# Turning the queries and keys of a three-layer attention kernel with one sixteen-block transposing DMA a visit

## The chip, the core and the metric

The kernel runs on one NeuronCore of a Trainium2 chip. The engines are PE (TensorE, matrix products), DVE (VectorE), ACT (ScalarE), POOL (GpSimd) and SP (SyncE, which here only issues DMAs). Each engine works through its own instructions in order, and they wait for one another by semaphores. The metric is the time of one execution on the device, in microseconds (us), lower being better.

## What is computed

Eight sequences of 128 tokens with 144 channels pass a rotation that depends on a condition vector, and then three transformer blocks with 16 heads of 9 channels and a hidden width of 576. Shifts, scales and gates of each block come from the same condition vector. Blocks 1 and 2 use a layer norm, block 3 an RMS norm, and block 3 also normalises queries and keys per head.

```python
x = _L0_cond_ref(x, cond, P, W, b)               # rotation: expm of a skew matrix, per sequence
...
h = _modulate(_layernorm(x), shift_msa, scale_msa)
qkv = (h @ W_qkv + b_qkv).reshape(b, l, 3, H, D)  # H = 16, D = 9
q, k, v = (qkv[:, :, 0], qkv[:, :, 1], qkv[:, :, 2])
scores = jnp.einsum('blhd,bmhd->bhlm', q * scale, k)
attn = jax.nn.softmax(scores, axis=-1)
o = jnp.einsum('bhlm,bmhd->blhd', attn, v).reshape(b, l, c)
x = x + gate_msa * (o @ W_proj + b_proj)
h = _modulate(_layernorm(x), shift_mlp, scale_mlp)
x = x + gate_mlp * (gelu(h @ W_fc1 + b_fc1) @ W_fc2 + b_fc2)
```

## The kernel before

The first third of the time is a preparation: loads, condition products, a matrix exponential and an orthogonalisation with one small step after another on DVE. After that come 24 **visits**, one for each sequence in each layer (visit v is sequence v % 8 of layer v // 8). Visits of equal parity share buffers (index h = v % 2).

**One visit.** TensorE turns the normalised tokens (`h_turn`) and makes queries, keys and values into PSUM bank 1 (`qkv`). Queries and keys are needed to better than bf16, so each number is written as three bf16 parts: ACT writes the first part (`first`, k = 0 for the queries and 1 for the keys), DVE the remainder (`residue`, `second_parts`, `third_parts`). The parts of a head pair fill one block of 128 by 128, so that a visit has 16 blocks, 8 of queries and 8 of keys. They lie in `brief` with the tokens on partitions and have to be turned, into `skw_r`, before `scores` can multiply them. `scores(v, g)` with g = 0 and g = 2 makes eight products each into banks 6 and 7, DVE takes the row maxima of every four heads (`maxima(v, 0)` to `maxima(v, 3)`), splits them (`max_high`, `max_low`), TensorE turns them (`max_turn`), and `scores_T` makes the transposed scores less the maxima; ACT takes the exponential (`exps`), `pv` multiplies with the values, `o_back`, `o_turn` and `proj` bring the result back, and the gated sum goes into x. The feed-forward half (`h2_turn`, `fc1`, `gelu`, `fc2`, `mlp_out`) is done for two visits at a time.

**How the blocks are turned.** Three ways share the 16 blocks. TensorE turns blocks 0 to 3 (queries of heads 0 to 7) by four transposing products into bank 6 (`parts_turn`, line 1309) and DVE copies them out (`q_out`, line 1971). SP turns blocks 12 to 15 by one DMA (line 375), which are the keys of heads 0 to 7, because the weights' columns are rolled by half the keys (`by_head` on the host). SP turns blocks 4 to 11 by a second DMA (line 376). `scores(v, 0)` needs the copy and the first DMA only, `scores(v, 2)` the second one. SP issues both when `third_parts` has signalled `parts_ready` and the buffer of two visits before is free.

**What sets the order.** The visits overlap. Each engine runs a loop over slots from -2 to 27, and a table written by hand lists, for each kind of slot (the first two, even and odd ones of layers 1 and 2, even and odd ones of layer 3, the last ones), which step of which visit stands next in the engine's queue: in slot s TensorE does `scores` of visit s, `scores_T` and `pv` of visit s - 1, `qkv` of visit s + 1, and so on. An even and an odd slot together are called a pair here; a pair is two visits. `stay_warm(n)` puts n products into the queue whose result is never read.

Of the kernel before, what the change touches and what calls it, by code (L numbers as in the profile page):

```python
# [37 lines left out]
H, HD = 16, 9  # L38
# [79 lines left out]
def program(nc, t, out, spread_mods):  # L118
    ctx = ExitStack()
    with ctx:  # L120
# [117 lines left out]
        qkT = [[both_turned[h][:, 8 * k:8 * k + 8, :] for h in range(2)] for k in range(2)]  # L238
# [55 lines left out]
        qT_full, qT_ready = sem("qT_full"), sem("qT_ready")  # L294
        keys_turned = [sem(f"keys_turned{h}") for h in range(2)]
# [30 lines left out]
        def _(sp):  # L326
# [85 lines left out]
        def _(pool):  # L412
# [189 lines left out]
            for slot in range(-2, VISITS + 4):  # L602
                if slot < 2 and slot % 2 == 0:
                    pair_at(second_half_tail, slot, 4, 0)
                    visit_at(first_deviation, slot + 2, start=2)
                    pair_at(mlp_add, slot, 6)
                    visit_at(attention_add, slot - 2)
                    visit_at(first_tail, slot + 2, start=2)
                    pair_at(second_half_tail, slot, 4, 1)
                elif slot < 2 and slot % 2 == 1:  # L610
                    pair_at(second_deviation, slot, 3)
# [3 lines left out]
                elif slot >= VISITS - 1 and slot % 2 == 0:  # L615
                    visit_at(last_parts, slot - 3, start=LAST)
                    visit_at(first_deviation, slot + 2, start=2)
                    pair_at(second_half_tail, slot, 4, 0)
                    pair_at(second_half_tail, slot, 4, 1)
                    visit_at(attention_add, slot - 2)  # L620
                    visit_at(first_tail, slot + 2, start=2)
                    visit_at(last_deviation, slot - 2, start=LAST)
                    pair_at(mlp_add, slot, 6)
                elif slot >= VISITS - 1 and slot % 2 == 1:
                    visit_at(first_deviation, slot + 2, start=2)
                    visit_at(last_parts, slot - 3, start=LAST)
                    visit_at(attention_add, slot - 2)
                    pair_at(second_deviation, slot, 3)
                    visit_at(first_tail, slot + 2, start=2)
# [1781 lines left out]
```

## Time and profile before

| | us |
|---|---|
| median of 3 runs | 363.49 |
| lowest and highest run | 363.12, 363.57 |
| the profiled execution, its whole time | 363.12 |
| its span, first to last instruction | 361.2 |
| PE, DVE, ACT, POOL busy in the span | 308.4, 293.4, 207.2, 166.2 |

The profiled execution took 1.9 us outside its span. The visits begin at about 113 us. Visits 2 to 15 (layers 1 and 2) run in pairs of 17.6 us until about 248 us, visits 16 to 23 (layer 3) in pairs of 20.6 to 20.7 us until about 331 us, and the rest is the end of the last visits.

How to read the rows: the name left of the arrow is what an instruction writes and the one right of it what it reads (`ps` is PSUM, `brief` the parts, `skw_r` the turned parts, `nmax` the maxima), L followed by a number is a line of the kernel (L1016 is a helper for most products, L375 and L376 are the two transposing DMAs), and xN is how often. PEld is the load of a product's stationary operand. SPq is SP's queue.

### The profile page before, as it was taken

The page shows a single profiled execution, that of the slowest core. Times are in us where ns is not written, and L with a number is a line of the kernel's source. Part 1 is how long each engine was busy: PE and PEld are TensorE (multiplying, and loading weights), DVE is VectorE, ACT ScalarE, POOL GpSimd, SP SyncE. Part 2 cuts the span into 40 slices and gives each one's busy share as a digit, 9 for nine tenths or more (in the row PEclk, how much of TensorE's full clock was granted, in tenths as well). Part 3 has the DMA queues.
Part 4 walks back from the last instruction along what each step waited for, and adds up shares of the span by engine and source line. Part 5 has one row for each costly group of instructions (what it writes and reads, how often), then busy time and mean ns, then how long its engine had stood idle before and what let it go on. Part 6 is the DMA issues. An engine that isn't in the chain of part 4 may idle for free.

```text
span 361.2 us, 10726 instructions
## 1 busy us (share of the span) xinstructions
PE 308.4 (85%) x3494; PEld 211.6 (59%) x3502; DVE 293.4 (81%) x1511; ACT 207.2 (57%) x460; POOL 166.2 (46%) x536
## 2 busy tenths in 40 slices
PE   1969983983668998799999999999999998989896
PEld 0924721472124455486878777777666675766675
DVE  4999999999995678787888888787989888887632
ACT  4145110244011365688888887888686867768552
POOL 5424332356553322535354545454646646452442
PEclk9987655697699999999999999999999999999999
DMA  4797400039300233223222222222023222223101
GB/s 147 185 255 234 126 1 0 4 80 291 117 1 0 45 60 76 45 45 46 45 44 48 45 45 48 44 47 46 15 45 32 45 47 45 45 41 37 34 16 34
DMA packets 48735, 23.58 MB, mean 65 GB/s; under 512 B 40186, under 2 KB 47198, under 8 KB 48552
## 3 DMA queue, kind: packets, MB, share of 16 engines
q1 hardware_dynamic: 48680, 22.89, 27.8%
q8 instruction: 29, 0.48, 0.5%
q14 instruction: 26, 0.21, 0.2%
HBM read 12.82 MB, written 0.62 MB: 37 GB/s over the span
## 4 chain that ended last, share of the span: by engine, by line
PE 42%; DVE 39%; issue 8%; DMA 4%; POOL 3%; SPq 1%; ACT 1%; POOLq 0%; DVEq 0%
PE ps L1016 34%; DMA skw_r<-brief 4%; DVE grow L1647 4%; DVE nmax L1976 3%; DVE top L1702 3%; DVE trow L1647 3%; PE ps L1415 3%; DVE beta L1681 3%; DVE den L1687 2%; DVE tfac L1695 2%; DVE lead L1669 2%; DVE late L1669 2%; PE ps L1309 1%; DVE gfac L1663 1%; DVE grec L1659 1%
## 5 line engine op out<-in xcount | busy, mean ns | idle before, releaser
L1976 DVE TENSOR_REDUCE nmax<-ps 128x4 f32<-128x512 f32 x96 | 63.4, 683 | 11.7 <-PE ps L1016 11.4
L796 ACT ACTIVATE skw_t<-ps 128x512 f32<-128x512 f32 x96 | 52.0, 595 | 14.8 <-PE ps L1016 14.2
L448 POOL TENSOR_TENSOR root<-grow,half 32x1 f32<-32x1 f32 x64 | 34.6, 542 | 54.0 <-DVE grow L1647 53.6
L1016 PE MATMUL ps<-skw_r 54*128 54x128 bf16 x768 | 43.5, 217 | 4.7 <-DMA skw_r<-brief 2.3
L1016 PEld LDWEIGHTS ps<-skw_r 54*128 54x128 bf16 x768 | 30.4, 94 | 20.8 <-issue 11.5
L1016 PE MATMUL ps<-mT_t,fc1w_t 128*128 128x256 f32 (+1 forms) x130 | 36.0, 379 | 0.0
L1016 PE MATMUL ps<-fc2w,skw_r 128*128 128x144 f32 (+1 forms) x240 | 34.7, 292 | 0.0
L1016 PE MATMUL ps<-sel,identb 128*128 128x512 bf16 x83 | 23.7, 404 | 9.6 <-DVE grow L1647 8.6
L1016 PEld LDWEIGHTS ps<-fc2w,skw_r 128*128 128x128 f32 (+1 forms) x240 | 30.8, 190 | 1.6 <-issue 0.2
L1016 PE MATMUL ps<-nmT,sel 64*128 64x128 bf16 x384 | 27.6, 216 | 0.0
L813 ACT ACT_TABLE_LOAD x21 | 26.9, 1283 | 0.4
L562 POOL TENSOR_TENSOR rstd<-vare,nhalf 128x1 f32<-128x1 f32 x24 | 13.2, 552 | 28.8 <-DVE vare L2075 18.6
L548 POOL TENSOR_TENSOR tail<-ln,gmod 128x16 f32<-128x16 f32 x48 | 12.0, 250 | 29.3 <-DVE ln L1883 23.9
L1016 PEld LDWEIGHTS ps<-mT_t,fc1w_t 128*128 128x128 f32 x130 | 18.9, 190 | 5.9 <-issue 2.0
L1016 PE MATMUL ps<-qkvw_t,hT_t 128*128 128x432 f32 x48 | 22.3, 545 | 0.0
L557 POOL TENSOR_TENSOR x<-x,skw_r 128x144 f32<-128x144 f32 x24 | 11.8, 490 | 22.4 <-DVE skw_r L2025 22.4
L790 ACT ACTIVATE brief<-ps 128x432 bf16<-128x432 f32 x32 | 16.9, 562 | 7.8 <-PE ps L1016 7.8
L1016 PE MATMUL ps<-skw_t,brief 128*32 128x128 f32 x512 | 19.8, 278 | 1.0 <-DVE skw_r L2025 0.4
L1016 PEld LDWEIGHTS ps<-sel,identb 128*128 128x128 bf16 x91 | 7.7, 101 | 21.1 <-DVE grow L1647 9.3
L828 ACT ACTIVATE skw_r<-ps 128x512 f32<-128x512 f32 (+1 forms) x33 | 16.7, 515 | 5.8 <-PE ps L1016 5.7
L1016 PEld LDWEIGHTS ps<-nmT,sel 64*128 64x128 bf16 x384 | 19.6, 94 | 0.0
L803 ACT ACTIVATE skw_t<-ps 128x512 f32<-128x512 f32 x24 | 14.0, 583 | 7.0 <-PE ps L1016 6.9
(273 smaller groups left out, 815.4 us busy)
## 6 DMA issues: line engine op xcount, KB each, us to landing
gmod<-spread_mods SPq DMA_DIRECT2D x3, 1408.0 KB, 13.2
adaw_t<-in_ada SPq DMA_DIRECT2D x3, 432.0 KB
tails<-in_tail SPq DMA_DIRECT2D x3, 427.1 KB
skw_t<-in_skw SPq DMA_DIRECT2D x1, 1024.0 KB
fc1w_t<-in_fc SPq DMA_DIRECT2D x3, 320.0 KB
fc2w<-in_fc SPq DMA_DIRECT2D x3, 288.0 KB
skw_r<-brief SPq DMA_TRANSPOSE x48, 3.1
qkvw_t<-in_qkv SPq DMA_DIRECT2D x3, 216.0 KB
```

The source lines that it names most:

```text
L448: g.tensor_tensor(root[:, p, j:j + 1], grow[:, i % 4, 0:1], half[:], ALU.pow).then_inc(root_ready, 1)
L548: step(g.tensor_tensor(y[:], ln[kind][h][:, 128:C], m[:, CT:2 * CT], ALU.mult))
L562: g.tensor_tensor(rstd[:, 0, h:h + 1], vare[:, 0, h:h + 1], nhalf[:, 0:1], ALU.pow).then_inc(rstd1, 1)
L790: a.activation(dst, src, ACT.Copy).then_inc(first_parts, 1)
L796: a.activation(prob[g].rearrange("p i t -> p (i t)"), ps[:, 2 + g % 2, :], ACT.Exp, scale=SCALE).then_inc(prob_ready, 1)
L803: a.activation(o_raw[v % 2].rearrange("p g t -> p (g t)"), ps[:, 4, :], ACT.Copy).then_inc(o_raw_ready, 1)
L813: a.activation(table_out[:], half[:], f).then_inc(table_used, 1)
L828: a.activation(hid[0:rows, 2 * r:2 * r + n, :, :].rearrange("p c h t -> p (c h t)"), ps[0:rows, FC1_BANKS[r], 0:n * 2 * T], f).then_inc(hi ...
L1016: return pe.matmul(o, lhsT, rhs, start=start, stop=stop, skip_group_check=True)
L1647: return d.stream_shuffle(out_, rows, [j] * HALF)
L1669: i = d.scalar_tensor_tensor(out=elim[p][:, w], in0=grow[:, (HALF * p + j) % 4, 1:D + 1], scalar=gfac[:, p, j:j + 1], in1=elim[p][:, w], o ...
L1976: d.tensor_reduce(nmax[:, v % 2, first:first + 7:2], ps[:, 6 + g % 2, :].rearrange("p (i t) -> p i t", i=4), AX_X, ALU.max, negate=True).t ...
```

## The change

All 16 blocks of a visit are turned by one DMA. The four transposing products of TensorE, the copy of DVE, the rolled key columns and the semaphores `qT_full`, `qT_ready` and `keys_turned` are gone. `scores(v, 0)` now waits for the whole DMA, and `scores(v, 2)` for nothing more. `first` waits for the DMA of two visits before instead of its three sources. The unread products before the first scores fall from 8 and 8 to 6 and 2, and the two before `parts_turn(1)` go. The tables of all slots are rewritten on all four engines.

```diff
@@ -372,8 +371,7 @@
                 sp.wait_ge(parts_ready, v + 1)
                 if v >= 2:
                     sp.wait_ge(sT_full, 4 * (v - 2) + 4)
-                sp.dma_start_transpose(both_turned[h][:, 12:16, :], both_parts[h][:, 12 * T:16 * T]).then_inc(keys_turned[h], 16)
-                sp.dma_start_transpose(both_turned[h][:, 4:12, :], both_parts[h][:, 4 * T:12 * T]).then_inc(turned[h], 16)
+                sp.dma_start_transpose(both_turned[h], both_parts[h]).then_inc(turned[h], 16)
...
@@ -776,10 +774,6 @@
                 if v >= 2:
-                    if k == 0:
-                        act.wait_ge(qT_full, v - 1)
-                    else:
-                        act.wait_ge(keys_turned[h], 16 * (v // 2))
                     act.wait_ge(turned[h], 16 * (v // 2))
...
@@ -1300,16 +1294,6 @@
-            def parts_turn(v):
-                if v == 1:
-                    stay_warm(2)
-                o = refill(6, qT_ready, v + 1).bitcast(BF16)
-                pe.wait_ge(parts_ready, v + 1)
-                for pair in range(H // 4):
-                    i = pe.transpose(o[:, pair * T:(pair + 1) * T],
-                                     parts[0][v % 2][:, 2 * pair:2 * pair + 2, :].rearrange("p h d -> p (h d)"), identb[:])
-                i.then_inc(qT_full, 1)
-
...
@@ -1359,13 +1343,10 @@
             def scores(v, g):
                 if v == 0:
-                    stay_warm(8)
+                    stay_warm(6 - 2 * g)
                 if v == 1:
                     stay_warm(1 + g)
                 if g == 0:
-                    pe.wait_ge(qT_ready, v + 1)
-                    pe.wait_ge(keys_turned[v % 2], 16 * (v // 2 + 1))
-                else:
                     pe.wait_ge(turned[v % 2], 16 * (v // 2 + 1))
...
@@ -1964,12 +1937,6 @@
-            def q_out(v):
-                dve.wait_ge(qT_full, v + 1)
-                if v >= 2:
-                    dve.wait_ge(sT_full, 4 * (v - 2) + 4)
-                d.tensor_copy(qkT[0][v % 2][:, 0:4, :].rearrange("p k t -> p (k t)"), ps[:, 6, :].bitcast(BF16)[:, 0:4 * T]).then_inc(qT_ready, 1)
-
```

One entry of the tables, of DVE's even slots in layers 1 and 2, shows how the orders move:

```diff
...
                 elif slot % 2 == 0:
                     visit_at(input_stats, slot + 3, start=2)
-                    visit_at(input_means, slot + 3, start=2)
+                    visit_at(residue, slot + 1, start=1)
+                    visit_at(gated, slot - 2)
                     visit_at(maxima, slot, 0)
...
```

TensorE's queue in an even slot of layers 1 and 2, before: the turned maxima (L1385), the tokens, the four transposes (L1309), then eight products of `scores_T` (read from `skw_r` and `nmT`) and `o_back` (L1415).

```order
397 L1385 MATMUL ps<-identb,nmp 128x128
398 L1251 MATMUL ps<-ident,ln 128x128
399 L1241 MATMUL ps<-identb,tailp 102x128
400 L1309 MATMUL ps<-identb,brief 128x128 x4
401 L1016 MATMUL ps<-skw_r 128x128 x2
```

Further on in the same slot, before: the end of `scores_T`, then `scores(v, 0)` (the row of x8), then `proj`.

```order
420 L1016 MATMUL ps<-skw_r 128x128 x2
421 L1016 MATMUL ps<-nmT,sel 128x128 x2
422 L1016 MATMUL ps<-skw_r 128x128 x8
423 L1016 MATMUL ps<-projw_t,x_t 128x144
424 L1016 MATMUL ps<-projw_u,x_t 128x144
```

The same two places in one piece, after.

```order
412 L1010 MATMUL ps<-skw_r 128x128 x2
413 L1010 MATMUL ps<-nmT,sel 128x128 x2
414 L1010 MATMUL ps<-projw_t,x_t 128x144
415 L1010 MATMUL ps<-projw_u,x_t 128x144
416 L1010 MATMUL ps<-skw_r 128x128 x8
```

The four transposes are gone, and `scores(v, 0)` stands behind `proj` instead of ahead of it; odd slots are changed in the same way.

DVE's queue in an odd slot of layers 1 and 2, before, from the second maxima to the parts of the next visit: `maxima` (L1976), the statistics of `second_input` (L1864 to L1870), two `maxima`, `residue` (L1953), `max_high` (L1989), `second_parts` (L1960), `max_low` (L1994), `third_parts` (L1965).

```order
962 L1976 TENSOR_REDUCE nmax<-ps 128x4
963 L1864 BN_STATS st<-x 128x6 x2
964 L1867 BN_AGGR st<-st 128x2 x2
965 L1870 TENSOR_SCALAR vare<-st 128x2
966 L1976 TENSOR_REDUCE nmax<-ps 128x4 x2
967 L1953 TENSOR_TENSOR res<-ps,brief 128x288
968 L1989 CAST nmp<-nmax 128x2x8
969 L1960 CAST brief<-res 128x16x2x9
970 L1960 CAST brief<-res 128x16x18
971 L1994 TENSOR_TENSOR nmp<-nmax,nmp 128x2x8
972 L1965 TENSOR_TENSOR brief<-res,brief 128x2x16x9
```

The same place, after.

```order
944 L1943 TENSOR_REDUCE nmax<-ps 128x4 x2
945 L1837 BN_STATS st<-x 128x6 x2
946 L1840 BN_AGGR st<-st 128x2 x2
947 L1843 TENSOR_SCALAR vare<-st 128x2
948 L1943 TENSOR_REDUCE nmax<-ps 128x4
949 L1926 TENSOR_TENSOR res<-ps,brief 128x288
950 L1933 CAST brief<-res 128x16x2x9
951 L1933 CAST brief<-res 128x16x18
952 L1938 TENSOR_TENSOR brief<-res,brief 128x2x16x9
953 L1943 TENSOR_REDUCE nmax<-ps 128x4
```

The parts of the next visit are finished ahead of the fourth maxima and of their split; in even slots they stand behind the first two maxima both before and after.

## Rows read from the trace of the kernel before

**Rows 1.** Windows, one pair each; columns: us, busy time by engine, PEclk, DMA

```profile
177.60:195.20 17.60, 17.38 (x241) 13.41 (x240) 14.38 (x48) 14.83 (x32) 8.81 (x30) 1.00 0.24 48
...
289.60:310.30 20.70, 19.15 (x242) 13.81 (x244) 18.34 (x68) 15.54 (x35) 11.84 (x40) 1.00 0.20 40
```

**Rows 2.** The chain of waits, from 130 us; columns: start, duration, what

```profile
141.36 4.96 DMA skw_r<-brief
...
160.08 6.92 PE ps L1016 x107
...
178.34 6.92 PE ps L1016 x107
...
195.94 6.92 PE ps L1016 x107
...
281.25 4.62 DMA skw_r<-brief
...
289.53 0.30 PE ps L1236
...
310.23 0.30 PE ps L1236
```

**Rows 3.** Groups by line and form, 141 to 246 us (12 visits)

```profile
L1309 PE MATMUL ps<-identb,brief 128*128 128x128 bf16 x47 | 4.6, 219 | 0.0
L1971 DVE COPY skw_r<-ps 128x512 bf16<-128x512 bf16 x12 | 5.0, 415 | 0.0
```

**Rows 4.** The two DMAs by source line, all visits: duration of the issue, landing

```profile
L375 SPq DMA_TRANSPOSE skw_r<-brief x24: 1189/1191/1309, 120.9 to 330.7; - x24
...
DMA to landing us min/median/max: 2.4/2.4/4.3
```

**Rows 5.** The same for the DMA of eight blocks

```profile
L376 SPq DMA_TRANSPOSE skw_r<-brief x24: 1297/1312/2483, 122.2 to 332.0; - x24
...
  PEld ps L1016: 6.6, 8
...
DMA to landing us min/median/max: 3.1/3.2/5.0
```

**Rows 6.** DMA windows of one visit's two transfers; columns as in rows 1

```profile
203.90:204.70 0.80, 0.80 (x11) 0.69 (x6) 0.41 (x3) 0.75 (x3) 0.53 (x3) 1.00 0.81 164
205.10:206.70 1.60, 1.48 (x28) 0.88 (x26) 1.20 (x7) 1.17 (x4) 1.23 (x7) 1.00 0.86 164
```

**Rows 7.** Timeline of an odd and an even slot; columns: start, duration, instruction

```profile
196.40 0.40 PE L1016 MATMUL ps<-skw_r 54*128 54x128 bf16 x8
...
198.44 0.52 DVE L1864 BATCH_NORM_STATS2 st<-x 128x6 f32<-128x144 f32 x2
...
202.24 0.46 DVE L1965 TENSOR_TENSOR brief<-res,brief 128x288 bf16<-128x288 f32 x1
...
202.73 1.19 SPq L375 DMA_TRANSPOSE skw_r<-brief  x1
...
203.96 1.31 SPq L376 DMA_TRANSPOSE skw_r<-brief  x1
...
206.50 0.39 PE L1016 MATMUL ps<-skw_r 54*128 54x128 bf16 x8
...
206.92 0.69 DVE L1976 TENSOR_REDUCE nmax<-ps 128x4 f32<-128x512 f32 x1 [0.56 <-PE ps L1016]
...
209.50 0.45 DVE L1965 TENSOR_TENSOR brief<-res,brief 128x288 bf16<-128x288 f32 x1
```

**Rows 8.** Landing of single visits: line 375 at 133.4, line 376 at 332.0

```profile
DMA to landing us min/median/max: 3.1/3.1/3.1
...
DMA to landing us min/median/max: 4.0/4.0/4.0
```

**Rows 9.** Timeline of TensorE, first visits

```profile
123.49 0.40 PE L1016 MATMUL ps<-skw_r 54*128 54x128 bf16 x8 [0.40 <-issue]
...
125.65 0.40 PE L1016 MATMUL ps<-skw_r 54*128 54x128 bf16 x8
```

More of the change, by code:

```diff
@@ new lines, in _ @@
+                    pair_at(mlp_add, slot, 6)
+                    visit_at(last_parts, slot - 2, start=LAST)
+                elif slot >= VISITS - 1 and slot % 2 == 1:
+                    visit_at(first_tail, slot + 2, start=2)
+                    visit_at(attention_add, slot - 2)
+                    visit_at(first_deviation, slot + 2, start=2)
+                    visit_at(last_deviation, slot - 2, start=LAST)
+                    visit_at(last_parts, slot - 2, start=LAST)
+                elif (slot + 1) // B == 2 and slot % 2 == 0:
+                    pair_at(second_deviation, slot, 4)
@@ L995, in _ @@
                     pair_at(gelu, slot, 4, 0)
-                    pair_at(gelu, slot, 4, 1)
-                    visit_at(v_out, slot + 1, start=1)
-                else:
+                else:
+                    pair_at(gelu, slot, 5, 1)
+                    visit_at(v_out, slot, start=1)
                     pair_at(gelu, slot, 5, 2)
@@ L1008, in _ @@
                     visit_at(exps, slot - 1, 3)
-                    visit_at(v_out, slot + 1, start=1)
                     visit_at(o_out, slot - 1)
@@ new lines, in _ @@
+                    visit_at(scores_T, slot - 1, 2)
+                    visit_at(scores, slot, 0)
+                    pair_at(fc1, slot, 4, 0)
+                    visit_at(pv, slot - 1, 2)
+                    pair_at(fc1, slot, 4, 1)
+                    visit_at(o_back, slot - 2)
+                    visit_at(scores, slot, 2)
+                    visit_at(proj, slot - 2)
+                    visit_at(pv, slot - 1, 3)
+                elif slot < 2 and slot % 2 == 1:
+                    visit_at(h_turn, slot + 1, start=2)
+                    visit_at(o_back, slot - 2)
+                    visit_at(qkv, slot + 1, start=1)
+                    pair_at(fc1, slot, 5, 2)
+                    visit_at(max_turn, slot - 1)
+                    pair_at(fc2, slot, 5, 0)
+                    visit_at(scores, slot, 0)
+                    visit_at(scores_T, slot - 1, 0)
+                    visit_at(scores_T, slot - 1, 2)
+                    visit_at(scores, slot, 2)
@@ L1443, in _ @@
                     visit_at(pv, slot - 1, 0)
                     visit_at(pv, slot - 1, 1)
+                    visit_at(o_turn, slot - 2)
+                    pair_at(fc2, slot, 5, 1)
+                    visit_at(proj, slot - 2)
+                    visit_at(pv, slot - 1, 2)
+                    visit_at(pv, slot - 1, 3)
+                elif slot >= VISITS - 1 and slot % 2 == 0:
+                    visit_at(scores, slot, 0)
+                    visit_at(h_turn, slot + 1, start=2)
+                    visit_at(o_back, slot - 2)
@@ L2156, in _ @@
                     visit_at(attended, slot - 1)
[L2157 removed]
+                    pair_at(second_input, slot, 3)
+                    visit_at(gated, slot - 2)
                 elif slot >= VISITS - 1 and slot % 2 == 0:
+                    visit_at(next_normal, slot + 2, start=2)
                     visit_at(input_stats, slot + 3, start=2)
[L2160 to L2161 removed]
+                    visit_at(residue, slot + 1, start=1)
```

418 lines of the change are left out of this document (179 added, 239 removed).

## Prediction

> **What bounds the kernel now.** I read the busy time by stretch first. In a pair of layers 1 and 2 TensorE is busy 17.38 of 17.60 us, DVE 14.38, ACT 14.83 [rows 1]: TensorE is the bound. In a pair of layer 3 TensorE is busy 19.15 and DVE 18.34 of 20.70 us [rows 1]: neither is full, and the chain of waits runs from one to the other and through POOL. The granted clock is 1.00 in both. The chain of waits then gives the lengths. The same piece of TensorE work starts at 160.08, 178.34 and 195.94, so one pair took 18.26 us and the next 17.60 [rows 2]; in layer 3 the mark at 289.53 comes again at 310.23, 20.70 us later [rows 2]. Last I read what each transposing DMA takes, since the change rests on that.
>
> **The transfer.** The DMA of four blocks lands 2.4 us after its issue began (median), that of eight 3.1 us [rows 4, 5]. The second is issued 1.23 us after the first (202.73 and 203.96 [rows 7]), so all blocks are there 4.3 to 4.4 us after the parts are ready. In the windows the packets of the four blocks fill 0.8 us from 1.17 us after the issue, those of the eight 1.5 to 1.6 us, at 164 GB/s over each window [rows 6]; the landing is about 0.5 us after the last packet. Sixteen blocks by the step from four to eight (0.7 us for four blocks): 3.1 + 2 x 0.7 = 4.5. By the windows: 1.2 + 2 x 1.5 + 0.5 = 4.7. I take 4.6 us, with bounds of 4.2 (one start-up less than the two windows hold) and 5.0. So the last block comes 0.2 us later than now, but the operands of `scores(v, 0)` come at 4.6 instead of 2.4.
>
> **A page's rate.** By the packets the transposing transfers ran at 164 GB/s over the windows [rows 6]. The Trainium skill, Advanced Engine Details and Errata, section X-Bar Transpose (TRN2), expects 350 to 400 GB/s of such a transfer. By that the 524 kB of sixteen blocks would take about 1.4 us and land after some 3.1 us (an estimate from that page and the start and end above), and no wait named below would be left. The rows say 164, and I go by them.
>
> **What is removed.** Per visit the four transposing products go. Their group shows 4.6 us for 47 of them in twelve visits, 0.38 us a visit with the pipeline's tail, which the next product overlaps [rows 3]; their starts are about 0.06 us apart, 0.24 us for four. I take 0.25 us of TensorE a visit, 0.5 a pair, between 0.5 and 0.8. DVE loses the copy, 0.415 us a visit [rows 3]: worth nothing in layers 1 and 2, where DVE idles 3.2 us a pair, and up to 0.8 us a pair in layer 3. SP loses one issue of 1.3 us a visit, which delays nobody now but the landing already counted.
>
> **Layers 1 and 2.** TensorE alone would make the pair 17.60 - 0.5 = 17.1 us. Moving `proj` ahead of `scores(v, 0)` may add 0.1 us a slot, because `proj` waits for ACT's copy and the scores used to fill that gap; moving `max_turn` up takes the same back from the wait for the turned maxima. I put both at nothing. Now the other loop, by which parts go to the DMA, the DMA to the scores, and DVE reaches the next parts only behind the maxima of these scores. In an even slot the scores start at 206.50, the first maxima at 206.92 [rows 7], so 0.42 us; then two maxima of 0.65, two casts in 0.52 and `third_parts` 0.45: 2.8 us from landing to issue. In an odd slot `second_input` (about 1.05 us from 198.44 [rows 7]), the third maxima and `residue` stand between as well: 0.42 + 1.3 + 1.05 + 0.9 (the third maxima, with its wait for the second scores) + 0.45 + 1.0 = 5.1 to 5.2 us. With two landings: 2.8 + 5.2 + 2 x 4.6 = 17.2 us. Before, the same loop was 206.50 to 209.95, 196.40 to 202.70 [rows 7] and twice 2.44: 14.6 us, which leaves 3.0 us of slack in a pair of 17.6. **This slack is what hides a late transfer today, and the change spends all of it.** The pair becomes 17.2 us, a gain of 0.4; for seven pairs -2.8 us.
>
> **Late transfers.** They are common. Read visit by visit, ten of the 24 visits have a landing at least 0.7 us over the median of its kind; the first is 3.1 instead of 2.4 at visit 2, the last 4.0 instead of 3.1 at visit 23 [rows 8], the largest 4.3 instead of 2.4 and 5.0 instead of 3.1 [rows 4, 5]. By the larger of a visit's two excesses they sum to 12.6 us, 5.9 of it in visits 2 to 15 and 6.7 in layer 3. What of it is paid now: the 4.96 us landing at 141.36 is on the chain, 1.8 us over the median, and the pair from 160.08 is 0.66 us over its neighbour [rows 2]: 2.5 us. In layer 3 the 4.62 at 281.25 is on the chain too [rows 2], but pairs with and without such a piece are equally long, so I count nothing as paid. In all, the weight loads waited 6.6 us for the second DMA in eight cases [rows 5]. With a loop of 17.2 against TensorE's 17.1 a late landing is paid in full. How many will be late is the unknown. The excess is no property of the transposes' own length (fourteen visits have none), so the same number of delays met by a transfer that is 0.3 us longer in all bounds it near 12.6; half of it if the moved transfers miss what they met before. I take two thirds, 8.4 us, less 2.5 paid now: **+5.9 us** (bounds +3.8 and +10.1; 0 or below if the landings are clean).
>
> **Layer 3.** The same loop: even slot 0.42 + 1.3 + `unit_parts` 0.52 + ACT's `first` with its wait 1.3 + 0.45 + 1.1 = 5.1; odd slot, with `second_normal`, the other two maxima and their split, 6.1; with two landings 5.1 + 6.1 + 9.2 = 20.4 us against 20.70 now. TensorE falls to 18.65 and DVE to 17.5, so neither takes over. I take -0.25 us a pair, -1.0 for four, between -3.2 (the copy of DVE and the transposes in full) and +1.
>
> **The first and the last visits.** Visit 0 has its first scores at 123.49 and the second at 125.65, as the second DMA lands [rows 9]. Now both start at about 125.4, behind the whole transfer, and two `maxima` of 0.65 us that ran between them come after: +1.3, less the unread products of 0.4 us that also go, +0.9 us. The two `parts_turn` of the start, 0.25 each less what waits cover, give back 0.2. Sum +0.7, between -0.5 and +1.5. The end needs the last blocks of visit 23, whose DMA lands 4.0 us after 332.0 [rows 8], that is 5.3 after the parts; 4.6 to 6 then, at no cost and no gain. `gelu` and `v_out` cross into the next slot on ACT, which idles 2.8 us a pair, and `attention_add` goes behind `first_tail` on POOL, which is half idle: nothing, since `second_input` comes later on DVE; if that cover is gone, 0.5 us of POOL's add appears once a pair.
>
> **The sum.** -2.8 - 1.0 + 0.7 + 5.9 = +2.8 us on the profiled execution, 361.2 of span and 1.9 around it, 363.12 in all: 365.9. The median is 0.37 above that execution, so I predict **366.3 us**.
>
> **The rivals.**
>
> *Clean landings, faster.* If the sixteen blocks land after 4.6 us or less nearly always, the late term is not +5.9 but -2.5, since today's delays go too: -2.8 - 1.0 + 0.7 - 2.5 = -5.6, **357.9 us**; with a third of the excess (+1.7 net) it is about 362. For it speaks that fourteen of 24 visits have no delay, that one DMA can be hit only once, and that both full engines lose work. It decides at a late excess of about 5.6 us in all: below, the kernel is faster. A landing of 4.2 us adds 0.8 us of slack a pair and has the same effect. The skill's rate, above, would end here as well.
>
> *Even, no change.* Half of the excess is met (6.3 - 2.5 = +3.8): -2.8 - 1.0 + 0.7 + 3.8 = +0.7, **364.2 us**, and with a little less it is 363.5.
>
> *Full exposure.* All of the 12.6 us is paid: -2.8 - 1.0 + 0.7 + 10.1 = +7.0, **370.5 us**. A landing of 5.0 us would do the same: 0.8 us a pair in eleven pairs, +8.8. Against it: the queue orders have been moved so that parts come earlier and scores later, which the loop sums above may hold by 0.3 us too high.
>
> **How the numbers follow.** Two executions of this kernel differ by about 0.2%, 0.7 us, and less than that can't be told from no change. The forecast with full exposure, that is slower by over 0.2%: 0.48, of it 0.12 for above 369. Even: 0.14. Clean landings, faster by over 0.2%: 0.38. The slower case alone spans 364.3 to 371. Because both signs hold much, the range takes in both: it reaches from 358.5, which leaves out some 0.09 of the clean end, to 371.0, which leaves out 0.06 above.
>
> **What would show it.** The transposing DMA: 24 issues of about 1.5 us, landing at 4.6 in the median (4.2 and 5.0 decide for the rivals), and a maximum near 6. The forecast is right if the weight loads' waits for that DMA grow from 6.6 us to over 12 in all, and pairs of layers 1 and 2 fall apart into some of 17.2 us and some of 18 to 19. It is wrong if all of them are 17.2 or less, with those waits under 4 us: then the parts come earlier than my loop has them. DVE should be 10 us less busy, TensorE 6 to 10 less. If layer 3's pairs leave 20.4 by more than 1 us in either direction, the step on layer 3 has failed; if the first scores of visit 0 start before 125 us, the landing has.

## The result and the profile after

The changed kernel takes **383.80 us** (median of 4 runs, 380.32 to 385.62), the kernel before in its company 363.31 us (363.12 to 363.57): ratio **1.055**, 95% interval 1.051 to 1.058 (here and below a ratio leaves out runs over 1.5% above the fastest of the same kernel, a median takes in all). I had said 366.3 us and at most 371. The direction was right, the size was not. The profiled execution took 384.43 us with a span of 382.6 us, 21.4 us more than before.

Where do the 21.4 us lie? The issue of a visit's first transposing DMA is a good mark. That of visit 3 comes 7.1 us later than before (147.3 for 140.1 us), the stretch from there to visit 15 is 7.7 us longer (112.7 for 105.0), that from visit 15 to 23 is 5.5 us longer (91.1 for 85.6), and the rest adds 1.1. So there are three questions: first visits, pairs of layers 1 and 2, layer 3.

First the page, the busy time and granted clock of the changed kernel:

```profile
PE 316.5 (83%) x3396; PEld 211.7 (55%) x3396; DVE 288.2 (75%) x1487; ACT 207.4 (54%) x460; POOL 163.6 (43%) x536
...
PEclk9988555895999669799999999999999999989999
```

TensorE lost its 96 transposing products and is busy 8.1 us longer than before. The dips to 6, 6 and 7 behind 124 us and to 8 behind 335 us are part of the answer: in the kernel before, the clock was 1.00 throughout these stretches.

The DMA by its source line, which answers [rows 4, 5]:

```profile
L374 SPq DMA_TRANSPOSE skw_r<-brief x24: 1784/1912/3107, 121.1 to 351.1; - x24
...
  PEld ps L1010: 11.1, 11
  PE ps L1010: 8.3, 7
...
DMA to landing us min/median/max: 4.2/4.3/6.0
```

The median landing is 4.3 us, 0.3 less than forecast, with a tail to 6.0. TensorE's products stood idle for it seven times, its weight loads waited eleven times, eight of them in visits 16 to 23, that is in every visit of layer 3.

**First visits.** The timeline of TensorE (idle time before the instruction in brackets), then all stretches of the changed kernel behind 120 us in which the granted clock was 0.50 (the column before the last two):

```profile
125.46 0.40 PE L1010 MATMUL ps<-skw_r 54*128 54x128 bf16 x8 [2.95 <-DMA skw_r<-brief]
127.33 0.61 PE L1010 MATMUL ps<-skw_r 54*128 54x128 bf16 x8 [0.93 <-DVE nmax L1943]
```

```profile
127.37:141.02 13.65, 11.46 (x105) 6.69 (x105) 6.93 (x21) 5.10 (x12) 2.41 (x8) 0.50 0.23 44
151.26:158.09 6.83, 6.65 (x71) 3.60 (x69) 5.37 (x16) 3.23 (x7) 2.07 (x7) 0.50 0.01 2
335.58:338.99 3.41, 3.17 (x31) 2.59 (x32) 2.90 (x10) 2.03 (x4) 2.10 (x9) 0.50 0.00 0
```

The first scores start at 125.46, as forecast (125.4; before at 123.49 [rows 9]). But TensorE had stood still for 2.95 us, and soon after it ran for 13.7 us at the lower of its two levels (1.2 instead of 2.4 GHz). The same happens at 151 us, behind a wait of 1.69 us for the split maxima, and at 336 us in layer 3.

**Pairs of layers 1 and 2.** Marks from the chain of waits, a window of one pair (answers [rows 1, 2]), and the only waits of TensorE's products over 0.2 us in it:

```profile
177.99 1.69 PE ps L1010 x19
...
196.82 1.69 PE ps L1010 x19
```

```profile
177.99:196.82 18.83, 17.79 (x235) 13.22 (x236) 14.09 (x45) 14.63 (x32) 8.72 (x30) 1.00 0.30 58
```

```profile
180.69 0.48 PE L1010 MATMUL ps<-projw_t,x_t 128*128 128x144 f32 x2 [0.23 <-ACT x_t L829]
196.06 0.22 PE L1366 MATMUL ps<-identb,nmp 128*128 128x128 bf16 x1 [0.81 <-DVE nmp L1961]
```

A pair is 18.83 us long instead of 17.60, and no DMA is among the waits: one waits for ACT's copy in front of `proj`, one for the split maxima in front of `max_turn`. Of the 1.23 us, 0.41 is busy time (17.79 for 17.38) and 0.82 idle time of TensorE.

**Layer 3.** The chain of waits has the late landings in it:

```profile
304.88 5.99 DMA skw_r<-brief
...
317.28 5.66 DMA skw_r<-brief
...
328.00 5.90 DMA skw_r<-brief
```

TensorE waited 4.4 us for these three, 1.48 of it in visit 21:

```profile
333.95 0.34 PE L1010 MATMUL ps<-skw_r 54*128 54x128 bf16 x6 [1.48 <-DMA skw_r<-brief]
```

Behind this one the clock falls for 3.4 us (the third window above). In each of the visits 16 to 22 the first scores start at most 0.06 us behind the landing, so that here, unlike in layers 1 and 2, the landing is in the loop and a late one is paid in full. The pairs from issue to issue are 20.9, 22.0 and 24.4 us, against 20.5 to 20.8 before.

### The profile page after: what moved, and what is told of

Same layout as the page of the kernel before. It is cut to its first block, busy times and chain, and to the rows that moved or that the text cites. A ratio compares the mean times of both kernels' runs of the same rounds, so it can differ in the third digit from the quotient of the medians.

```text
span 382.6 us, 10388 instructions
## 1 busy us (share of the span) xinstructions
PE 316.5 (83%) x3396; PEld 211.7 (55%) x3396; DVE 288.2 (75%) x1487; ACT 207.4 (54%) x460; POOL 163.6 (43%) x536
## 4 chain that ended last, share of the span: by engine, by line
DVE 38%; PE 38%; DMA 11%; issue 7%; ACT 3%; POOL 2%; SPq 1%; POOLq 0%; ACTq 0%; DVEq 0%
PE ps L1010 32%; DMA skw_r<-brief 10%; DVE nmax L1943 5%; DVE grow L1620 3%; DVE top L1675 3%; DVE trow L1620 3%; DVE beta L1654 2%; PE ps L1396 2%; DVE den L1660 2%; DVE tfac L1668 2%; DVE brief L1933 2%; DVE late L1642 2%; DMA tmask<-in_tmask 1%; DVE lead L1642 1%; DVE tnum L1661 1%
## 5 line engine op out<-in xcount | busy, mean ns | idle before, releaser
L1943 DVE TENSOR_REDUCE nmax<-ps 128x4 f32<-128x512 f32 x96 | 62.3, 684 | 14.4 <-PE ps L1010 13.9
L1010 PE MATMUL ps<-skw_r 54*128 54x128 bf16 x768 | 47.7, 226 | 14.8 <-DMA skw_r<-brief 8.3
L1010 PEld LDWEIGHTS ps<-skw_r 54*128 54x128 bf16 x768 | 30.8, 98 | 33.5 <-DMA skw_r<-brief 11.1
L1010 PE MATMUL ps<-fc2w,skw_r 128*128 128x144 f32 (+1 forms) x240 | 35.6, 297 | 0.0
L1010 PEld LDWEIGHTS ps<-fc2w,skw_r 128*128 128x128 f32 (+1 forms) x240 | 31.9, 194 | 3.9 <-issue 3.3
L1010 PE MATMUL ps<-nmT,sel 64*128 64x128 bf16 x384 | 28.8, 222 | 0.0
L546 POOL TENSOR_TENSOR tail<-ln,gmod 128x16 f32<-128x16 f32 x48 | 11.0, 228 | 37.8 <-DVE ln L1856 28.4
L1010 PE MATMUL ps<-qkvw_t,hT_t 128*128 128x432 f32 x48 | 25.1, 606 | 0.8 <-issue 0.8
L1010 PE MATMUL ps<-skw_t,brief 128*32 128x128 f32 x512 | 20.6, 287 | 0.4
L822 ACT ACTIVATE skw_r<-ps 128x512 f32<-128x512 f32 (+1 forms) x33 | 17.1, 517 | 7.1 <-PE ps L1010 7.1
L836 ACT ACTIVATE hT_t<-ps,mod_t 128x128 f32<-128x128 f32 x24 | 10.9, 455 | 14.1 <-PE ps L1235 14.1
```

The source lines that it names most:

```text
L822: a.activation(hid[0:rows, 2 * r:2 * r + n, :, :].rearrange("p c h t -> p (c h t)"), ps[0:rows, FC1_BANKS[r], 0:n * 2 * T], f).then_inc(hi ...
L1010: return pe.matmul(o, lhsT, rhs, start=start, stop=stop, skip_group_check=True)
L1943: d.tensor_reduce(nmax[:, v % 2, first:first + 7:2], ps[:, 6 + g % 2, :].rearrange("p (i t) -> p i t", i=4), AX_X, ALU.max, negate=True).t ...
```

## The experiments

The comparison with the kernel before is in each case with its runs in the same company (medians 362.2 to 364.0 us). Two theories stood at the start: the orders cost the time (A), or the longer transfer does (B).

**1. Only the fills of the first visits.**

```diff
-                    stay_warm(6 - 2 * g)
+                    stay_warm(20 - 7 * g)
```

> The changed kernel with more unread products ahead of the first scores (20 and 13 instead of 6 and 2), so that TensorE works through the 2.9 us and 0.9 us it idled behind the first transfer. Theory clock: the idle time at 122.5 to 125.5 us let the granted clock fall to 0.5 until 140 us and again at 150 us; with it filled the clock stays at 1.00, and of the 7.2 us that visit 3's transfer starts later than before, about 4 come back: 379 to 380 us. Theory transfer (the first visits are late because each waits for its whole transfer, whatever the clock): 383 us, unchanged.

381.57 us, ratio 1.049 (1.044 to 1.054), 17.6 us above before instead of 20.5. The DMA of visit 3 is issued at 142.8 instead of 147.3 us, so the fall of the clock behind visit 0 had cost 4.5 us. A second fall from 145 us on takes a part of it back, and the total stays 1.6 us above the 379 to 380 us that I had expected. Idle TensorE and the clock behind it are shown as the cause of the first part.

**2. Only DVE's odd table:** `max_high` and `max_low` ahead of `mlp_out`, among the parts.

```diff
+                    visit_at(maxima, slot, 3)
                     visit_at(residue, slot + 1, start=1)
+                    visit_at(max_high, slot)
                     visit_at(second_parts, slot + 1, start=1)
+                    visit_at(max_low, slot)
                     visit_at(third_parts, slot + 1, start=1)
-                    visit_at(maxima, slot, 3)
                     pair_at(mlp_out, slot, 5)
-                    visit_at(max_high, slot)
-                    visit_at(max_low, slot)
```

> The changed kernel with one table changed: in DVE's odd slots of layers 1 and 2 the fourth maxima and the split of the maxima stand again ahead of and between the steps that write the parts, as before the change. Theory queue: TensorE's max_turn waited 0.8 us a pair for the split, and scores_T and all behind it with it; pairs go from 18.84 to 17.6 or less and the whole to about 376 us. Theory transfer: parts are now ready 0.7 us later, the transfer lands behind the place of the scores, and the pair stays near 18.8: 383 us.

380.02 us, ratio 1.042 (1.036 to 1.048). Pairs of 18.4 us: the wait of 0.81 us for the maxima was worth 0.44 us a pair. The 0.8 us that are left above 17.60 have another cause.

**3. The old orders with the one DMA of sixteen blocks.**

```diff
-                sp.dma_start_transpose(both_turned[h][:, 12:16, :], both_parts[h][:, 12 * T:16 * T]).then_inc(keys_turned[h], 16)
-                sp.dma_start_transpose(both_turned[h][:, 4:12, :], both_parts[h][:, 4 * T:12 * T]).then_inc(turned[h], 16)
+                sp.dma_start_transpose(both_turned[h], both_parts[h]).then_inc(turned[h], 16)
```

> The kernel before with all its orders as they were, and only the transposition changed: one DMA of sixteen blocks, no transposes by TensorE, no copy by DVE. Theory orders (most of the 20 us is from the rewritten tables): faster than the changed kernel, 366 to 372 us, and pairs of layers 1 and 2 at 17.6 to 18.2. Theory transfer (the landing of 4.3 us itself costs the 20 us, and the new tables soften it): slower than 384 us, pairs over 19 us.

**397.58 us**, ratio 1.090 (1.082 to 1.097). Theory A in its simple form fell: the new orders are worth 14 us. The chain of waits of one pair shows why:

```profile
200.76 4.28 DMA skw_r<-brief
...
205.08 3.60 PE ps L1009 x33
...
211.41 4.26 DMA skw_r<-brief
...
219.20 4.35 DMA skw_r<-brief
```

From 200.76 to 219.20 is 18.44 us, with two landings in it and 9.9 us of other steps. The kernel before had the same loop at 14.6 us, 9.8 us beside two landings of 2.4. Lengthening each by 1.9 gives 18.4. The 14 us that the new orders give back don't lie in these pairs (18.83 us with them) but mostly in layer 3: from the issue of visit 16 to that of visit 22 experiment 3 takes 78.2 us, the changed kernel 67.3, the kernel before 62.0. A part of that is the clock: around waits of 1.98, 2.94 and 2.99 us TensorE ran at 1.2 GHz for 6.8, 6.8 and 10.2 us there, and in the changed kernel for 3.4.

**4. Experiments 1 and 2 together.**

> The changed kernel with both edits, more unread products at the start and the split of the maxima first. If the two causes are independent, the gains add: 383.8 - 4 - 7.5 = about 372 us. If the clock's fall comes from later waits as well, less than the sum.

377.86 us and not 372, ratio 1.038 (1.033 to 1.043). A window of one pair, and the wait at its start:

```profile
209.50:227.90 18.40, 17.73 (x231) 13.20 (x232) 13.44 (x45) 14.62 (x33) 8.75 (x31) 1.00 0.31 60
```

```profile
209.50 0.63 PE L1396 MATMUL ps<-ident,skw_t 128*128 128x128 f32 x4 [0.44 <-ACT skw_t L797]
```

No DMA is waited for, and still 18.40 us. The new order has `o_back` in front of `scores_T(v, 0)` and waits there for ACT's copy, and TensorE's own busy time is 0.35 us longer than before [rows 1], although four blocks a visit are gone.

**5. The old orders with a short first transfer.** The eight blocks of the first scores become neighbours (the queries' columns are rolled, not the keys') and go first. The diff is against experiment 3.

```diff
-                sp.dma_start_transpose(both_turned[h], both_parts[h]).then_inc(turned[h], 16)
+                sp.dma_start_transpose(both_turned[h][:, 4:12, :], both_parts[h][:, 4 * T:12 * T]).then_inc(eight_turned[h], 16)
+                sp.dma_start_transpose(both_turned[h][:, 0:4, :], both_parts[h][:, 0:4 * T]).then_inc(turned[h], 16)
+                sp.dma_start_transpose(both_turned[h][:, 12:16, :], both_parts[h][:, 12 * T:16 * T]).then_inc(turned[h], 16)
```

> The kernel before with all its orders; no block is turned by TensorE, and the sixteen go in three transposing DMAs: the eight blocks that scores(v, 0) needs first (the queries' columns are rolled so that they are neighbours), then four, then four. Theory that the landing in front of the first scores is the direct cost: with an 8-block landing of 3.1 us instead of 4.3 the DMA loop is 14.6 + 2 x (3.1 - 2.4) = 16.0 us a pair, under TensorE's own work of about 17.1, so pairs of layers 1 and 2 come to 17.1-17.4 us and the kernel to 358-364 us. Rival, that TensorE's transposes were needed whatever the DMA's length is (SyncE's queue now issues three DMAs of 1.2 us, and the last blocks come late for scores(v, 2)): pairs stay at 18 us or more and the kernel above 370 us.

367.31 us, ratio 1.010 (1.004 to 1.016): 30 us less than experiment 3 with the same work on TensorE. This is the strongest single piece of evidence for theory B: in the old orders the length of the first landing is the cost. A window of a pair, and a group in it with TensorE's idle time before it:

```profile
178.85:196.29 17.44, 17.01 (x235) 12.88 (x235) 13.80 (x44) 14.84 (x32) 8.80 (x31) 1.00 0.34 63
```

```profile
L1013 PE MATMUL ps<-skw_r 54*128 54x128 bf16 x66 | 3.7, 217 | 0.2 <-DVE nmT L1972 0.2
```

The pair is 17.44 us. TensorE's busy time fell by 0.37 us, the pair by 0.16: the turned blocks had covered the wait of `scores_T` for the turned maxima, which now shows with 0.2 us. The pair had been expected at 17.1 to 17.4 us, the total at 358 to 364, and that it missed. Most of the loss, 3.5 of 5.9 us in the profiled execution, lies in one place of layer 3, visit 19 to 20, 15.2 us for 11.7. Timeline and window there:

```profile
294.50 0.40 PE L1013 MATMUL ps<-skw_r 54*128 54x128 bf16 x8 [1.66 <-DMA skw_r<-brief]
```

```profile
297.00:301.00 4.00, 4.00 (x42) 3.54 (x34) 2.39 (x9) 2.14 (x4) 1.45 (x5) 0.50 0.00 0
```

The landing was late (4.6 for 3.3 us), TensorE stood 1.66 us, and behind it ran at 1.2 GHz. A wait of 1.36 us in visit 21 was followed by no such fall. In layer 3 of the changed kernel waits of 1.57 and 1.33 us were not either, but one of 1.48 us was.

**6. The new orders with the short first transfer** (experiment 4 with the three DMAs of experiment 5).

> The changed kernel with the longer fills and the split ahead of mlp_out (as in the run with both), all new orders kept, but with the eight blocks for scores(v, 0) in a DMA of their own, then four and four. Theory that the new orders of TensorE are what costs 0.8 us a pair in layers 1 and 2 and the transfer no longer does: pairs stay at 18.3-18.5 us there; only the first visits and the late landings of layer 3 gain, 3-6 us, so 372-375 us. Theory that the landing still costs directly: pairs fall to 17.6 us or less, and the kernel to 366 us or less.

373.67 us, ratio 1.028 (1.025 to 1.032). The window of a pair, and the group of the `qkv` products in it, then that group of the kernel before (178 to 195 us):

```profile
182.49:200.89 18.40, 17.73 (x233) 13.20 (x235) 13.45 (x44) 14.62 (x32) 8.75 (x31) 1.00 0.31 59
```

```profile
L1014 PE MATMUL ps<-qkvw_t,hT_t 128*128 128x432 f32 x4 | 2.0, 578 | 0.0
```

```profile
L1016 PE MATMUL ps<-qkvw_t,hT_t 128*128 128x432 f32 x4 | 1.8, 526 | 0.0
```

18.40 us, to the hundredth what experiment 4 had with landings 1 us longer. So in layers 1 and 2 the landing costs the changed kernel nothing directly; its orders cost 0.8 us a pair. Between 5 and 6 nothing but the orders and the fills differs: 17.44 against 18.40 us. Part of it is that the same products are slower in another neighbourhood: `qkv` takes 578 ns on average, 526 before. Product by product, the first of each two takes 630 ns directly behind a bf16 product (so it stands in the new orders) and 526 to 528 behind an f32 one (so it stood before); the second takes 523 to 526 in both. That is 0.2 of the 0.72 us by which TensorE's busy time differs between 5 and 6 (17.01 and 17.73). The shorter landing gave 3 to 4 us, outside these pairs.

**7. Experiment 4 with `scores_T(v, 0)` ahead of `o_back`.**

```diff
-                    visit_at(o_back, slot - 2)
                     visit_at(scores_T, slot - 1, 0)
+                    visit_at(o_back, slot - 2)
```

> The run with both edits, and in TensorE's even slots of layers 1 and 2 scores_T 0 stands ahead of o_back again, as in the kernel before; one DMA of sixteen blocks. If o_back ahead of scores_T 0 costs the wait for ScalarE's copy of o_raw (0.44 us and its tail, about 0.6 a pair), pairs come to 17.8 us from 18.4 and the kernel to 374 us from 377.9. If TensorE's wait only moves elsewhere, pairs stay at 18.3-18.5 and the time within 1 us of 377.9.

377.97 us (runs of 373.63, 375.90, 380.04 and 381.22), ratio 1.031 (1.026 to 1.037) from the two lower ones, 1.038 in experiment 4. The median moved by nothing, while the two lower runs lie 2 to 4 us below it; four runs so far apart don't size the gain in total. The pair of the profiled execution gained 0.19 us, not 0.6. The window and the group that tells why:

```profile
182.06:200.27 18.21, 17.62 (x234) 13.12 (x236) 13.56 (x44) 14.62 (x32) 8.76 (x31) 1.00 0.31 60
```

```profile
L1010 PE MATMUL ps<-skw_r 54*128 54x128 bf16 x66 | 4.0, 218 | 0.4 <-DVE nmT L1967 0.4
```

The wait for ACT (0.44 us) became one for the turned maxima (0.4 us). My expectation had looked at the wait that is there, not at the one behind it.

**8. Also `scores(v, 0)` ahead of `proj`, in both slots.**

```diff
-                    visit_at(proj, slot - 2)
                     visit_at(scores, slot, 0)
+                    visit_at(proj, slot - 2)
```

> As the run before it, and in both slots of layers 1 and 2 scores(v, 0) stands ahead of proj, so that proj has its cover again and the sixteen-block DMA has about 0.8 us less of it. If the order around proj is free while the landing keeps its margin of 0.8 and 0.5 us: pairs of 17.3-17.5 us, kernel 371 us. If the landing becomes the bound: pairs of 18 us or more with the DMA on the chain of waits, and the kernel at or above the run before it, 374 us or more.

378.68 us, ratio 1.044 (1.040 to 1.048), the second case of the expectation. The chain of waits:

```profile
180.79 4.25 DMA skw_r<-brief
...
185.09 3.60 PE ps L1010 x33
...
191.41 4.65 DMA skw_r<-brief
...
199.70 4.26 DMA skw_r<-brief
```

Pairs of 18.50 us with two landings each and 10.0 us beside them: a loop as long as that of experiment 3 is back. The chain goes through TensorE's 33 products in the odd slot, and in the even one through `proj` to `gated`, which stands ahead of the maxima in DVE's new table. **So in layers 1 and 2 the two theories are one cause.** With scores early in TensorE's queue the sixteen-block landing bounds the pair at 18.5 us; with scores late enough to hide it, the steps moved ahead of them lose their cover, and TensorE needs 18.2 to 18.8 us.

**9. The kernel before with its two DMAs merged into one of twelve blocks**, TensorE's four kept: the landing alone.

```diff
-                sp.dma_start_transpose(both_turned[h][:, 12:16, :], both_parts[h][:, 12 * T:16 * T]).then_inc(keys_turned[h], 16)
-                sp.dma_start_transpose(both_turned[h][:, 4:12, :], both_parts[h][:, 4 * T:12 * T]).then_inc(turned[h], 16)
+                sp.dma_start_transpose(both_turned[h][:, 4:16, :], both_parts[h][:, 4 * T:16 * T]).then_inc(turned[h], 16)
```

> The kernel before with every order and TensorE's four turned blocks kept; only its two transposing DMAs are merged into one of twelve blocks, which scores(v, 0) awaits. It lengthens the landing in front of the first scores alone. From 3.2 us for eight blocks and 4.3 for sixteen, twelve land in 3.7. Theory of the loop (14.6 us a pair with 2.4 us landings, and twice whatever is added): 14.6 + 2 x 1.3 = 17.2 us, still under TensorE's 17.6, so pairs of layers 1 and 2 stay at 17.6-17.7 and the kernel within 363-367 us. Rival, that every microsecond of landing is felt: pairs of 18.5 us or more and 372 us or above.

371.36 us, ratio 1.022 (1.019 to 1.026). Landings of 3.7 us. Two pairs in windows, and the DMA's view of visit 8, which lies in the second (its execution took 374.5 us, the longest of the four; the windows shown have the clock at 1.00):

```profile
162.76:180.36 17.60, 17.38 (x240) 13.42 (x241) 14.38 (x47) 14.85 (x32) 8.86 (x31) 1.00 0.24 47
180.36:199.40 19.04, 17.56 (x240) 13.44 (x241) 14.38 (x47) 14.84 (x33) 8.86 (x31) 1.00 0.23 43
```

```profile
q8 instruction: 1, 0.02, 1.1%
...
skw_r<-brief SPq DMA_TRANSPOSE x1, 5.1
```

In steady pairs the loop holds to 0.01 us: 17.2 us lie under TensorE's 17.60, so 1.3 us more of landing are free. With one late landing (5.1 us) the pair pays 1.44 us. In total the upper end of my expectation was 4 us too low: in the profiled execution layer 3 has no such slack (pairs of 21.7 to 24.1 us, with landings of up to 5.3 us and two stretches of 3.4 us at 1.2 GHz), and the first visits lose 2.2 us by visit 3. That execution is 3.2 us longer than the median, so these losses are at the high end.

**What makes a landing late.** The DMA view of the changed kernel for visits 9 (landing 4.3) and 19 (6.0), from issue to 6 us later:

```profile
GB/s 0 0 0 0 0 0 0 36 208 224 215 210 212 212 210 218 215 220 217 217 217 193 200 217 57 0 0 0 0 0 0 0 0 0 0 0 0 0 0 0
...
q1 hardware_dynamic: 2080, 0.52, 46.0%
```

```profile
GB/s 0 0 0 0 0 0 0 24 186 222 224 210 213 207 207 218 217 218 213 217 215 200 183 222 144 7 114 0 0 0 0 0 0 0 0 0 0 0 0 0
...
q8 instruction: 1, 0.02, 1.0%
q14 instruction: 1, 0.01, 0.4%
```

In visit 9 all 2080 packets are of the transfer's queue. In visit 19 there are two more, of queues that the profile calls `instruction`. I went through the 96 visits of the four sixteen-block kernels (the changed one, experiments 4, 7, 8). In 46 no such packet starts between issue and landing: they land after 4.2 to 4.4 us. In 50 at least one does: 25 of them land after 4.9 to 6.1 us, 25 after 4.2 to 4.7. All 20 landings over 5.0 us are among them. Experiments 1 to 3, with 72 more visits, show the same: at most 4.5 us in the 32 without such a packet, and all 13 landings over 5.0 us in the 40 with one. The kernel before has its own 4.3 us landing [rows 4] in such a place too. This is a coincidence in many places, not an intervention: I found no way to move these packets alone.

**10. Experiment 5 with fills before the late waits of layer 3.**

```diff
+                if g == 0 and v in (18, 19, 21, 23):
+                    pe.wait_ge(*reader[6])
+                    for r in range(4):
+                        mm(ps[:, 6, :], identb[:], sel[:, 4 * r:4 * r + 4, :])
```

> The run with the old orders and the eight blocks first, plus four 512-column fills (0.9 us) ahead of the wait for that DMA in visits 18, 19, 21 and 23, in which it landed late. Theory that visit 19's late landing of 4.6 us costs twice, by TensorE's wait of 1.7 us and by the clock at 0.50 for the 8 us behind it: with the fills the clock stays at 1.00 and the 4 us between issues 19 and 20 come back, 362-364.5 us in all. If the clock falls all the same, or the fills stand in the way of work: 366-368 us.

368.88 us, ratio 1.017 (1.014 to 1.020), the second case. The chain of waits:

```profile
269.19 4.78 DMA skw_r<-brief
...
292.91 4.62 DMA skw_r<-brief
```

Visit 17 is late now, where it was 3.0 us in experiment 5, and has no fill; visit 21 is on time. With the added code the instruction packets fall elsewhere: in visit 21 one starts 0.5 us before the issue, where it started 2.4 us behind it in experiment 5. In the total the gain is lost by this. Visit 19, though, answers the question, since its landing is 4.6 us in both:

```profile
297.00:301.00 4.00, 3.43 (x54) 2.88 (x55) 2.90 (x12) 1.41 (x4) 1.45 (x6) 1.00 0.28 52
```

The clock is 1.00 where it was 0.50, and visit 20 is issued 12.8 us behind visit 19 instead of 15.2. So with the same late landing the fall of the clock had cost 2.4 us, against the 4 that I had expected.

**11. Experiment 6 with six fills ahead of `max_turn(2)`.**

```diff
             def max_turn(v):
+                if v == 2:
+                    stay_warm(6)
```

> The run with the new orders and the eight blocks first, plus six fills (1.3 us) ahead of max_turn(2), where TensorE waited 1.7 us for VectorE's nmp and the clock then stood at 0.57 from 146 to 150 us. Theory that this fall costs 1.7 us and nothing else differs: 371.5-372.5 us against 373.7, transposes of visit 4 issued by 151.5 instead of 153.0, and pairs of layers 1 and 2 still at 18.4. Rival, that the chain there is VectorE's: no change, 373-374 us.

372.39 us (372.38 to 372.45), ratio 1.028 (1.025 to 1.030). Window by window, the one with 0.57 of clock in experiment 6 is:

```profile
146.00:150.00 4.00, 3.61 (x60) 2.33 (x63) 2.91 (x10) 2.87 (x7) 1.97 (x9) 1.00 0.45 57
```

The clock holds, but visit 4 is issued only 0.5 us earlier (152.5 for 153.0 us) and not 1.5. The median is 1.3 us lower, as expected, yet the kernel before was 1.1 us lower in this company too (362.17 for 363.26), and the two ratios can't be told apart. That fills keep the clock is shown here, a gain in time is not.

**12. The short first transfer in layer 2 alone**, the kernel before elsewhere. `by_dma(v)` is true for visits 8 to 15, and `parts_turn` and `q_out` do nothing there.

```diff
+                if by_dma(v):
+                    sp.dma_start_transpose(both_turned[h][:, 4:12, :], both_parts[h][:, 4 * T:12 * T]).then_inc(eight_turned[h], 16)
+                    sp.dma_start_transpose(both_turned[h][:, 0:4, :], both_parts[h][:, 0:4 * T]).then_inc(rest_turned[h], 16)
+                    sp.dma_start_transpose(both_turned[h][:, 12:16, :], both_parts[h][:, 12 * T:16 * T]).then_inc(rest_turned[h], 16)
+                    continue
```

> The kernel before, but in layer 2 alone (visits 8 to 15) no block is turned by TensorE: the eight blocks that the first scores need go in a DMA of their own, then four and four. The first visits and layer 3, in which every run so far lost by a longer landing, keep the old scheme. Theory that in the steady pairs the removed TensorE work is worth 0.16 us each (17.44 against 17.60) and the 3.2 us landing lies under the loop: 3.5 such pairs, 0.6 us, so 361.5-362.0 us where the kernel before has 362.2 in this company, ratio 0.997-0.999. If one of the layer's transfers meets an instruction fetch and lands above 4.5 us, that pair is 1.4 us longer: ratio 1.000-1.004. Below 0.996 or above 1.006 neither holds.

362.90 us against 362.87, ratio 1.000 (0.997 to 1.004), 12 and 17 runs. One of its pairs:

```profile
195.20:212.64 17.44, 17.01 (x233) 12.89 (x232) 13.80 (x45) 14.84 (x33) 8.86 (x30) 1.00 0.31 63
```

The 0.16 us a pair is there, and 3.5 times that can't be told from nothing. No version beats the kernel before.

## Why the prediction was wrong

**The transfer: right.** 4.3 us against 4.6. Packets ran at about 215 GB/s once they ran (the view above), faster than the 164 of my windows, which hold start and end. The 350 to 400 GB/s of the Trainium skill (Advanced Engine Details and Errata, section X-Bar Transpose (TRN2)) were reached in no transposing transfer here.

**What is removed: mis-sized.** 0.5 us a pair was booked. TensorE's busy time falls by 0.37, and 0.16 arrives (experiments 5 and 12), since the blocks had covered the turned maxima.

**Layers 1 and 2: the step that failed.** Forecast -2.8 us for seven pairs, measured +7.7 over six. The step is "TensorE alone would make the pair 17.60 - 0.5 = 17.1 us", with the moved `proj` and `max_turn` as "both at nothing". TensorE's own queue took 18.83 us, in a pair in which no DMA is waited for. DVE's odd table is 0.44 of the miss (experiment 2), and 0.8 us above the kernel before stay with the other orders, with landings of 4.3 us as with 3.2 (experiments 4 and 6); the rest is gain that I had taken off and that was not there. I never costed `o_back` ahead of `scores_T`, which was in the diff.

The loop, by contrast, was forecast well. An issue, the first scores behind it, the next issue, and so on through one odd and one even slot of the changed kernel:

```profile
202.86 1.98 SPq L374 DMA_TRANSPOSE skw_r<-brief  x1
207.69 0.40 PE L1010 MATMUL ps<-skw_r 54*128 54x128 bf16 x8
212.93 1.89 SPq L374 DMA_TRANSPOSE skw_r<-brief  x1
219.03 0.28 PE L1010 MATMUL ps<-skw_r 54*128 54x128 bf16 x3
221.71 3.08 SPq L374 DMA_TRANSPOSE skw_r<-brief  x1
```

From scores to issue it is 5.24 and 2.68 us, where I had 5.2 and 2.8. With two landings of 4.3 that is 16.4 us (forecast 17.2), and the scores start 0.6 and 1.8 us behind their landings, which is the slack of 2.4 us in 18.83. So the landing did not bound these pairs. The short steps hold only where the scores stand late: with the scores early they are 6.3 and 3.5 us in experiment 3, which has the old tables on all engines (so 9.8 + 2 x 4.3 = 18.4, which the rows of before told [rows 7]), and 6.3 and 3.6 in experiment 8. Early scores with DVE's tables just as in the changed kernel were not run.

**Late transfers: the right size in the wrong place.** I had 12.6 us of excess in before and took 8.4 as met. The excess over 4.3 us in the changed kernel is 8.4 in sum (visits 6, 13, 15, 19, 20, 21, 23). But it isn't paid in layers 1 and 2, since scores stand late in the queue there (0.7 us of waits), and is in layer 3 (4.4 us). I had also argued that delays are no matter of the transfer's length. Their number did not grow: by 0.6 us and more above the median, ten of 24 visits had a late landing before, in the first transfer or the second, and seven of 24 have one now. But only three of the ten were in the transfer for which the first scores wait, and now all seven are.

**Layer 3.** Forecast -1.0, measured +5.5 from visit 15 to 23. Here the loop is the bound, as forecast: 5.24 and 6.80 us from scores to issue (forecast 5.1 and 6.1) and landings of 4.3 and 4.5 make the 20.9 us of visits 16 to 18. The odd slot was 0.7 us too short in my sum. The waits for the three late landings are 4.4 us, and the fall of the clock behind the third is a cost of its own, which no run of the changed kernel separates (2.4 us for a longer one in experiment 10).

**First visits.** Forecast +0.7, measured +7.1. The start of the first scores was right to 0.1 us. Missing was the term for the clock: a stretch in which TensorE stands still for 2.95 us, with the fills cut from 8 and 8 to 6 and 2. I had booked these missing products as 0.4 us of gain. Experiment 1 gives 4.5 us of it. Not all that is left there is explained.

**The rivals.** Of the three none came true; full exposure (370.5 us) was nearest. What was missing among them is a rival in which the new orders lengthen TensorE's own queue, for 6 pairs 1.2 us each, with the clock beside it. Pairs of layers 1 and 2 did not fall apart into some of 17.2 us and some of 18 to 19: nearly all are 18.8. By my own sign the step on layer 3 failed too, as its pairs of 22.0 and 24.4 us leave 20.4 by more than 1. Of the signs, landing 4.6 and the weight loads' waits (11.1 us for "over 12") came near. "TensorE 6 to 10 us less busy" was wrong with the sign, 8.1 more, of which the stretches at 1.2 GHz and the new neighbourhood are the causes seen. DVE is 5.2 us less busy, not 10.

## What to carry to other kernels

Before a transfer is lengthened, write down the loop that it closes, landing by landing, from rows of the trace: with the orders kept, steps of 9.8 us plus two landings told 18.4 us before anything was run, and such a loop stays free as long as it lies under the engine's own time (experiment 9). Where the orders are rewritten as well, the steps of the loop can become shorter (7.9 us in the changed kernel), but then the engine's own queue is another one, and it has to be added up anew with its waits: here it took 18.83 us where 17.1 had been assumed. Work that a scheduler moves ahead of a late operand is not free filler: it loses its own cover, and each wait that is taken away uncovers the next one (experiments 5 and 7). Where an engine is made to stand still at the start of a phase, the clock of the stretch behind it belongs in the sum.

## What the hardware showed

- Transposing DMAs of 4, 8, 12 and 16 blocks of 128 x 128 bf16 landed after 2.4, 3.2, 3.7 and 4.3 us (medians): about 0.16 us a block behind a start of about 1.8. The queue of SP needs 1.2 us to issue one of four blocks and 1.9 to issue one of sixteen.
- Landings of sixteen-block transfers over 4.5 us, up to 6.1, came only where packets of the instruction queues (8 or 16 KB) started between issue and landing, and in about half of these cases the landing was not later than 4.7. That the packets are the cause is not shown. With a few instructions added they fell into other visits (experiment 10).
- TensorE ran at 1.2 GHz behind idle stretches of 2.95, 1.70, 1.66 and 1.48 us and not behind others of 1.57 and 1.36 us, so the length of the stop alone doesn't tell; the falls lasted 3.4 to 13.7 us. One of 6.8 us in layer 3 cost 2.4 us (experiment 10). Fills in front of the wait kept it at 2.4 GHz three times (experiments 1, 10 and 11).
- The same f32 product of 432 columns took 630 ns at full clock directly behind a bf16 product and 523 to 528 behind an f32 one, in the pairs of layers 1 and 2 shown for experiments 5 and 6.
